# Marked scatters, a nearer release of gathers, and pauses between gathers in an eight-layer graph kernel

## The reference

```python
# first layer, GNN                      # second layer, GNN
h = x @ W                               w = mlp(edge_attr8)             # three small matmuls per edge
e = exp(-leaky_relu(s[src] + t[dst]))   m = w * y[dst] * edge_attr4     # tensor products
out = relu(segsum(e * h[dst], src)      out = norm(segsum(m, src) @ w2 + x @ wsc)
           / segsum(e, src))
# third layer, GNN                      # fourth layer, GNN
l = (Q[dst] * K[src]).sum(-1) * scale   l = leaky_relu(es[src] + ed[dst])
w = segment_softmax(l, dst)             alpha = segment_softmax(l, dst)
out = segsum(w * V[src], dst) @ Wo ...  out = segsum(alpha * z[src], dst)
```

## Time and profile before

| | us |
|---|---|
| median of 3 runs | 5254.73 (5247.79 to 5256.63) |
| profiled execution, its own time | 5255.74 |
| its span | 5254.0 |
| PE busy | 3842.1 (73%) |
| DVE busy | 3228.2 (61%) |
| ACT busy | 2680.5 (51%) |
| POOL busy | 2558.2 (49%), 2689 instructions |

### The profile page before, as it was taken

The page is one execution under the profiler, slowest core; times in us unless marked ns, Lnnn a source line. Parts: engine busy times, 40 slices in busy tenths (PEclk is TensorE's granted clock), DMA queues, the critical chain, the costliest instruction groups (busy, mean ns, idle before and its releaser), DMA issues.

```text
span 5254.0 us, 74251 instructions
## 1 busy us (share of the span) xinstructions
PE 3842.1 (73%) x19152; PEld 2547.1 (48%) x19152; DVE 3228.2 (61%) x8314; ACT 2680.5 (51%) x8902; POOL 2558.2 (49%) x2689
## 2 busy tenths in 40 slices
PE   6868888626189999869666666678999946666665
PEld 2346666525044444458444445445655534444554
DVE  9955666543359899775667777753333435555753
ACT  6835777512068888744345656553233325555522
POOL 4666555656757687316155555521000056666244
PEclk9978899858589999989778888889999967777777
DMA  3023333334133333322455555520000033333334
GB/s 123 22 71 85 82 82 82 58 70 121 27 89 90 84 91 90 48 86 81 135 150 146 148 149 151 147 72 0 7 13 15 8 94 89 90 89 88 36 119 134
DMA packets 278821, 441.37 MB, mean 84 GB/s; under 512 B 114083, under 2 KB 192782, under 8 KB 278158
## 3 DMA queue, kind: packets, MB, share of 16 engines
q0 software_dynamic: 124624, 331.70, 24.7%
q1 hardware_dynamic: 147230, 98.37, 6.6%
q10 hardware_dynamic: 6560, 6.55, 0.4%
HBM read 368.84 MB, written 67.60 MB: 83 GB/s over the span
## 4 chain that ended last, share of the span: by engine, by line
PE 52%; DVE 18%; another core or an unknown queue 11%; issue 10%; ACT 5%; DMA 2%; DVEq 2%; POOL 1%; SPq 0%; ACTq 0%; POOLq 0%
PE PB L3178 7%; PE PB L2020 7%; PE PB L2554 5%; PE PB L726 5%; PE PB L1081 4%; PE PB L3162 3%; PE PB L1576 2%; ACT XNT L2638 2%; PE PB L2030 2%; PE PB L1564 2%; PE PB L1090 2%; PE PB L2042 1%; PE PB L2037 1%; DVE bigt L705 1%
## 5 line engine op out<-in xcount | busy, mean ns | idle before, releaser
L2554 PE MATMUL PB<-XNT 128*128 128x260 f32 x1760 | 617.7, 489 | 144.5 <-DVE bigt L2526 101.3
L1022 POOL DMA_INDIRECT bigt<-HTAB,bigt x440 | 421.1, 957 | 291.5 <-ACT bigt L1111 151.9
L2672 POOL DMA_INDIRECT bigt<-ZTAB,DO x440 | 454.7, 1033 | 220.8 <-issue 112.8
L1992 POOL DMA_INDIRECT bigt<-YTAB,bigt x440 | 472.2, 1073 | 177.5 <-issue 128.5
L359 POOL DMA_INDIRECT RECS<-bigt x391 | 389.8, 997 | 228.3 <-issue 94.4
L2554 PEld LDWEIGHTS PB<-XNT 128*128 128x128 f32 x1760 | 380.0, 238 | 217.4 <-issue 104.3
L717 ACT ACTIVATE bigt<-bigt 128x128 f16<-128x128 f16 x1214 | 383.3, 389 | 149.1 <-DVE bigt L690 62.5
L2638 ACT ACTIVATE XNT<-bigt 128x65 f32<-128x65 f32 x1768 | 446.2, 336 | 0.0
L2020 PE MATMUL PB<-bigt 128*128 128x512 f32 x880 | 407.9, 606 | 7.1 <-DVE bigt L2181 4.1
L726 PE MATMUL PB<-bigt 128*128 128x440 f16 x1564 | 366.9, 359 | 52.6 <-issue 30.4
L2672 POOL DMA_INDIRECT bigt<-KVTAB,DO x296 | 282.8, 955 | 243.5 <-DVE XNT L2434 157.6
(11 more groups left out here) (490 smaller groups left out, 9540.4 us busy)
## 6 DMA issues: line engine op xcount, KB each, us to landing
bigt<-YTAB,bigt POOLq DMA_INDIRECT x552
bigt<-SRT SPq DMA_DIRECT2D x56, 128.0 KB
OUTS<-bigt SPq DMA_DIRECT2D x56, 128.0 KB
SRT<-bigt SPq DMA_DIRECT2D x11, 640.0 KB, 9.9
bigt<-HTAB,bigt POOLq DMA_INDIRECT x440
bigt<-ZTAB,DO POOLq DMA_INDIRECT x440
KVTAB<-bigt SPq DMA_DIRECT2D x25, 258.0 KB
YTAB<-bigt SPq DMA_DIRECT2D x10, 640.0 KB, 10.1
```

The lines of the kernel that those rows point to most:

```text
L1022: e.indirect_dma_start(out=Gt[:, g % GB, j, :], out_offset=None, in_=HTAB, in_offset=bass.IndirectOffsetOnAxis(ap=SO[:, g * G + j:g * G + ...
L1992: e.indirect_dma_start(out=Gt[:, g % GB, j, :], out_offset=None, in_=YTAB, in_offset=bass.IndirectOffsetOnAxis(ap=SO[:, g * G + j:g * G + ...
L2554: m = e.matmul(self.PV[n % len(self.PV)], self.OH[:, g % self.MB, j, :], self.msg[:, g % self.MB, j, :], start=(k == 0), stop=(k == self.H ...
L2672: e.indirect_dma_start(out=dst[:, j, :], out_offset=None, in_=table, in_offset=bass.IndirectOffsetOnAxis(ap=DO[:, g * G + j:g * G + j + 1] ...
```

## The change

- The first sort issues 185 scatters instead of 150; scatter c waits for move 21c // 10 instead of 13c // 5. The stages between keep their counts, so 43 instead of 78 are left for the second layer's lead. There 18 are issued at once, and 25 each behind `turns.xnt` of one tile.
- In the first layer's loop the gathers of group g wait for the additions of group g - 7 (the same pair) instead of the weighing of group g - 8.
- In the third layer's loop, after every third gather, POOL runs `rest`: twice a memset of iotai[0:1, :] (one partition by 128 values) and a wait for its own mark.
- In the fourth layer's loop half n waits for the addition of half n - 29 instead of n - 32.

```diff
+        def rest(e):
+            for _ in range(2):
+                e.memset(iotai[0:1, :].bitcast(FP), 0.0).then_inc(Q.up(), 1)
+                e.wait_ge(*Q.now())
...
-                for c in range(150):
-                    e.wait_ge(*sort_s.rows_made.at(min(EC - 1, 13 * c // 5)))
+                for c in range(185):
+                    e.wait_ge(*sort_s.rows_made.at(min(EC - 1, 21 * c // 10)))
                     attr_scatters(e, 1)
...
                         if g >= GB and j % 2 == 0:
-                            e.wait_ge(*half(weighed, 2 * (g - GB) + j // 2))
+                            e.wait_ge(*half(added, 2 * (g - GB + 1) + j // 2))
...
             def pool(e):
+                attr_scatters(e, 18)
+                for t in range(NT):
+                    e.wait_ge(*turns.xnt.at(t))
+                    attr_scatters(e, 1)
                 attr_scatters(e, EC)
...
-        def gather_rows(e, dst, table, n, landed):
+        def gather_rows(e, dst, table, n, landed, run=0):
...
                 ).then_inc(landed, 16)
+                if run and (g * G + j) % run == run - 1:
+                    rest(e)
...
-                    gather_rows(e, slot(g), KVTAB, n, kv_in.sem(n))
+                    gather_rows(e, slot(g), KVTAB, n, kv_in.sem(n), 3)
...
-                        e.wait_ge(*att.added.at(n - 2 * GB))
+                        e.wait_ge(*att.added.at(n - 2 * GB + 3))
```

## The result

| | before | changed |
|---|---|---|
| median, us | 5252.18 (4 runs, 5247.79 to 5256.63) | 5215.85 (4 runs, 5208.89 to 5220.72) |
| profiled execution | 5255.74, span 5254.0 | 5211.38, span 5209.6 |

What follows compares the result with a forecast made beforehand. The prediction took PE's marks, late while POOL issues indirect DMAs back to back, as the bound. Lead -52, third loop -85, first loop -10, fourth loop 0 and sort +3 made -144 from 5255.7: 5111 us, range 5038 to 5232.

Steps and rivals of the forecast that it cites:

- The reading of the bound: Whole kernel: while POOL issues indirect DMAs back to back, PE's marks reach waiters late; a real pause lets them through.
- Sort: +3 forecast: First sort: 185 scatters at POOL's 1.25 us take 231 us, ending ahead of the first gather; +3 us.
- That cover holds if the pace does: First sort: scatters end before the first gather at 299.84 at POOL's pace; at the old 1.57 us each, +47.
- Lead: -52 forecast: Second layer's lead: turned tiles at best take 35.0 us, -57, less one stall of about 5.1 us; -52 us.
- Third loop: -85 forecast: Third layer's loop: rests cut ACT's 25 waits from 6.1 to 2.7 us each; -85, between -150 and +34.
- My input that a run's first four or so gathers let marks pass: Third layer's loop: PE's marks pass promptly during about four gathers at a run's start, shortening the wait behind a rest.
- First loop: -10 forecast: First layer's loop: the later wait hides and POOL's runs get shorter; -10 us, between -50 and +62.
- rival 2: POOL and additions in lockstep in the first loop, from a 6.57 us period, and rests only cost; +44, 5300; chance 0.10.
- My slack of 7.8 us: First layer's loop: time left for a group's last gather to land before DVE's logit reads it; 7.8 us.
- Fourth loop: 0 forecast: Fourth layer's loop: slack of 12.3 us still covers two gathers' 2.5 us; 0, between -15 and +20 us.
- rival 1: Third loop's rests let no mark through, only real waits do; -25 in all, 5231 (5200 to 5245); chance 0.20.
- My fourth rival: Third loop's 292 memsets hold DVE up, +58, and the lead gives only -25; 5289; chance 0.05.

Runs made afterwards that it cites:

- counts_2: Only the scatter counts (185 in the first sort, 18 and 25 marked in the lead) against the kernel before, late marks: 5333.8 us, ratio 1.0004.
- counts: Only the scatter counts (185 in the first sort, 18 and 25 marked in the lead) against the kernel before, no late marks: 4673.44 us, ratio 0.9902.
- unmarked: 185 scatters in the first sort, the lead's 43 issued at once without marks, against the kernel before, no late marks: 4669.69 us, ratio 0.9902.
- mild: 165 sort scatters, 12 more in first FFN, 18 + 25 marked + 8 in lead, waited third-loop rests, against before, late marks: 5299.24 us, 0.9937.
- all_rests: Waited rests after every third gather in the first, third and fourth layers' loops, against the kernel before, late marks: 5251.28 us, ratio 0.9862.
- first_loop_2: Only the first layer's gathers waiting for additions instead of weighings, against the kernel before, late marks: 5270.31 us, ratio 1.0026.
- fourth_loop: Only the fourth layer's gathers waiting for the addition 29 halves back instead of 32, against the kernel before, no late marks: 4717.86 us, ratio 1.0002.
- fourth_loop_2: Only the fourth layer's gathers waiting for the addition 29 halves back instead of 32, against the kernel before, late marks: 5334.45 us, ratio 1.0.
- no_wait: Only the third loop's rests, POOL not waiting for its two half-line memsets, against the kernel before, no late marks: 4720.01 us, ratio 1.0002.
- rests: Only the waited rests in the third layer's loop, against the kernel before, no late marks: 4732.15 us, ratio 1.003.

## Why the prediction was wrong, step by step

**The reading of the bound was right for this trace.** PE's marks are late where POOL issues back to back and on time where it stands: the waits of the earlier trace rows stayed with unwaited memsets (158.1 us) and went for the most part with waited ones (29.2 and 46.2 us). That the kernel takes 4719 us where no mark is late fits it, though the two kinds differ in more than the marks. The reading was right as far as it went; why marks are late in some runs and never in others it does not say.

**Sort: +3 forecast, +47.5 measured; the step that failed.** I wrote "That cover holds if the pace does", took POOL's own 1.25 us for the pace, and put the case in which a full POOL makes the sort's marks late at the far end, +47. It was the case. That the number fits is luck: I worked it out from the old pace of 1.57 us per scatter, while the 185 went out in 281.2 us, 1.53 us each, held up by a sort that itself had become slower. That the counts do this, and only with late marks, is shown: +50 in counts_2, +2 in counts. A scatter per 1.26 us on an engine that needs 1.27 has no pause left, and this follows from the reading on which the whole forecast rests. DVE's 235.00 busy us of 235.00 in the earlier trace rows, with a scatter per 1.57 us, were the hint that the sort's marks were on time and that its pauses kept it whole. The timeline of POOL and DVE in the changed kernel:

```profile
195.28 0.97 POOL L365 DMA_INDIRECT RECS<-bigt  x1 [0.30 <-issue]
196.55 0.97 POOL L365 DMA_INDIRECT RECS<-bigt  x1 [0.30 <-issue]
197.83 0.97 POOL L365 DMA_INDIRECT RECS<-bigt  x1 [0.30 <-issue]
201.23 0.96 POOL L365 DMA_INDIRECT RECS<-bigt  x1 [2.43 <-DVE bigt L711]
```
```profile
196.93 0.68 DVE L696 TENSOR_TENSOR bigt<-PB,bigt 128x512 f16<-128x512 f32 x1
199.08 0.45 DVE L711 TENSOR_SCALAR bigt<-PB,bigt 128x440 f16<-128x440 bf16 x1 [1.46 <-PE PB L732]
200.51 0.80 DVE L711 TENSOR_SCALAR bigt<-PB,bigt 128x440 f16<-128x440 bf16 x2 [0.98 <-PE PB L732]
```

DVE stands until POOL's run has ended (197.83 + 0.97 = 198.80), then goes on at 199.08.

**Lead: -52 forecast, -52.5 measured; how much of it the marks gave is not shown.** From the lead's first scatter (1339.1, now 1412.5) to the first gather (1475.6, now 1496.5) 136.5 us became 84. The turned tiles did what I forecast at best: 25 in 35.3 us instead of 91.9, with the table's way out 24.0 instead of 21.2 us behind them.

```profile
1437.09 0.38 ACT L474 ACTIVATE XNT<-PB 128x256 f32<-128x256 f32 x1 [9.53 <-issue]
...
1472.43 0.38 ACT L474 ACTIVATE XNT<-PB 128x256 f32<-128x256 f32 x1 [1.02 <-remote]
```

But two things were changed at once, the marks and the number. 35 scatters x 1.27 = 44.5 us are POOL's shorter queue, and in the prompt kind that is all of it (`unmarked`, -48 without a mark). In the late kind the shorter queue also ends the stretch in which tiles wait for late marks, so it may give most there too; if it counts in full, the marks are worth the other 8 us. `unmarked` did not run in the late kind, so I can't call my cause shown.

**Third loop: -85 forecast, -58 measured; the term was mis-sized.** ACT's waits on the transpose, the 153.7 us of the earlier trace rows, fell to 35.8 us (28.4 + 7.4), by 118 where I forecast 85, and yet the loop became only 58 us shorter. Two of its waits, and one of DVE's, from the loop's lists:

```profile
ACT bigt L2632 <- PE PB L2583: 26.3, 19, 6.8
...
ACT XNT L2641 <- remote: 21.6, 9, 6.9
```
```profile
DVE XNT L2457 <- remote: 30.0, 14, 5.0
```

But the same late marks now hold other waiters, in mild ACT's line 2641 for 77.3 us and DVE's line 2457 for 35.1. A set has several marks of PE in a row. I priced one waiter per set and took its freed time as the loop's. My input that a run's first four or so gathers let marks pass was too good as well: in before 23 to 60% of the marks in those places were late, and in all_rests, with runs of at most three, still 46 to 63%. That mild and all_rests gained 14 and 22 us where the change gained 58 stays open: the rests sat at the same gathers, the chip and the phase against PE differed, and each number is of one profile.

**First loop: -10 forecast, +28.5 measured; the second step that failed.** This was the first half of rival 2: its period went from 6.39 to (1091.6 - 366.9) / 109 = 6.65 us, over the 6.57 that I had set. My slack of 7.8 us was for the reader of the gathered rows, and that did hide: DVE's logits waited 5.1 us for gathers in all. I forecast shorter runs; they became longer. POOL's idle time at this wait rose from 151.9 us (behind weighings) to 202.3 (behind additions). Between pauses of over 1 us the gathers go out in eights in both kernels, but in before 33 short pauses of 0.4 to 1.0 us stand inside them, and in the change and in first_loop_2 no such pause is left. So the additions started POOL later and then let it run eight gathers on end:

```profile
712.64 0.95 POOL L1022 DMA_INDIRECT bigt<-HTAB,bigt  x1 [0.30 <-issue]
714.25 0.95 POOL L1022 DMA_INDIRECT bigt<-HTAB,bigt  x1 [0.66 <-issue]
```
```profile
755.61 0.96 POOL L1028 DMA_INDIRECT bigt<-HTAB,bigt  x1 [0.30 <-issue]
756.88 0.96 POOL L1028 DMA_INDIRECT bigt<-HTAB,bigt  x1 [0.30 <-DVE bigt L1180]
```

Which of the two, the later start or the lost pause, costs the 20 to 28 us is not shown; the share of late marks in the loop stayed (51 and 52%).

**Fourth loop: 0 forecast, +12.2 measured, not shown to be the edit's.** fourth_loop and fourth_loop_2 change nothing in the whole, and the loop has taken 672.6 to 687.1 us in late kernels that don't touch it.

**Second loop: 0 forecast, -15.4 measured, chance.** It takes either 681 to 683 or 697 to 713 us in late kernels, none of which touches it, with 2% or with 24 to 43% of late marks.

**The range** held since it reached to rival 1. Of the 100 us between the forecast's -144 and the -44 of the profiled pair the sort makes 44.5, the first loop 38.5 and the third 27; the rest of the stages differ by -10 in sum. My fourth rival, with the rule of the port pair from the Trainium skill's page "SBUF — State Buffer" beside it, found nothing to stand on: 292 memsets (each half as wide) cost nothing in no_wait, and the waited ones cost 13 us in rests, 0.09 us a pair, not 58.

## What to carry to other kernels

Where a trace shows PE's marks late in the runs of DMA issues on GpSimd, the pauses between the issues are a resource: count what is left of them before you put more issues into a stage that is still whole. Here filling it to the engine's own pace cost as much as the shorter queue gave elsewhere (+47 against -52; the counts alone gave 0 in the late kind). Price an edit in each kind of run that the kernel has: rests that give 81 us in the late kind cost about 172 in the prompt one, and the shorter lead is the one stretch that gave in both. And before you credit a mark for a shorter stretch, take only the marks away, in each kind. And look at whether the profiled execution is a typical one before you compare stages: mild's was the slowest of its ten.

## What the runs showed of the hardware that I had not expected

One kernel took 4719 and 5254 us, 11% apart, with the same instructions: without a single late mark of PE in the loops of the one kind, with half of them late in the other. In the late kind the share of late marks rises with the place in GpSimd's run of indirect DMAs, from 23% in the first to over 90% behind the sixth (before). Two waited memsets between gathers, 0.4 to 0.7 us more, freed most of one waiter's time (153.7 us to 29.2 and 46.2); two unwaited ones of 0.23 us in sum freed none (158.1). DVE's and ACT's recorded marks were on time in both kinds (0.01 us in the loops). A fifth of the marks has no record in the late traces, but who waits for DVE does not start later for it: ACT starts 35 ns behind DVE's end at the median with and without a record at that end. Behind PE it is 40 ns with one and 578 ns without. So what is late is PE's alone. What links PE's marks to GpSimd's runs is open, and no run here shows it.
